# Queries computed for two heads at once, and score maxima on two halves of TensorE's rows

## What is computed

```
xn = layernorm(x)
q = (xn @ Wq + bq)          # 16 heads of 64
k, v = xn @ Wk + bk, xn @ Wv + bv   # one key and value head of 64, shared by all 16
w = softmax(q_h . k / 8)    # 512 x 512 for each of 16 heads and 8 batch entries
x = x + concat(w @ v) @ Wo + bo + mixture_of_experts(xn)   # 8 experts, 2 chosen, 512 wide
```

## Time and profile before

| | |
|---|---|
| median of 3 executions | 1417.2 us (1414.25 to 1417.55) |
| the profiled execution | 1409.84 us, its span 1408.0 us |
| TensorE busy | 1286.0 us, 91% |
| VectorE busy | 1011.7 us, 72% |
| ScalarE busy | 708.6 us, 50% |
| GpSimd busy | 270.9 us, 19% |
| mean granted TensorE clock | 0.962 |

### The profile page before, as it was taken

One profiled execution on the slowest core, in us unless ns is written; L12 is line 12 of the kernel. 1 busy time (PEld: TensorE's weight loads), 2 busy tenths in 40 slices (PEclk: granted clock), 3 DMA queues, 4 the chain that ended last, 5 costly groups with the idle time before them and its releaser, 6 DMA issues.

```text
span 1408.0 us, 22235 instructions
## 1 busy us (share of the span) xinstructions
PE 1286.0 (91%) x7377; PEld 760.0 (54%) x7377; DVE 1011.7 (72%) x2393; ACT 708.6 (50%) x1300; POOL 270.9 (19%) x314
## 2 busy tenths in 40 slices
PE   4569988999989998999899999999999979999997
PEld 2335435554545555555454555555655538686844
DVE  7776866578857875787668766876687747677875
ACT  3126544544464445444554445544545448677741
POOL 3033222200120012001200120012000205454630
PEclk9569998999999999999999999999999989999999
DMA  2051433000210021003000200020000246465451
GB/s 75 0 158 61 151 108 138 29 17 19 84 32 17 18 85 32 18 18 85 31 17 19 85 32 17 18 85 32 18 17 19 62 136 207 155 214 170 144 179 48
DMA packets 69299, 100.25 MB, mean 71 GB/s; under 512 B 29196, under 2 KB 45132, under 8 KB 65220
## 3 DMA queue, kind: packets, MB, share of 16 engines
q1 hardware_dynamic: 54628, 66.23, 15.2%
q0 software_dynamic: 11344, 31.64, 6.9%
q10 hardware_dynamic: 3216, 0.97, 0.3%
HBM read 59.86 MB, written 38.68 MB: 70 GB/s over the span
## 4 chain that ended last, share of the span: by engine, by line
PE 73%; DVE 16%; issue 3%; DMA 2%; ACT 2%; SPq 2%; POOL 1%; DVEq 0%; ACTq 0%; POOLq 0%
PE bank L1420 14%; PE bank L1392 8%; PE bank L1348 7%; PE bank L1431 6%; PE bank L1393 6%; PE bank L1256 5%; PE bank L1258 5%; PE bank L1257 5%; PE bank L1452 4%; DVE mneg L987 3%; PE bank L1272 2%; PE bank L1262 2%; DVE q_lm L981 2%; PE bank L1307 2%; PE bank L1289 1%
## 5 line engine op out<-in xcount | busy, mean ns | idle before, releaser
L815 ACT ACTIVATE wide<-bank 128x512 f32<-128x512 f32 x512 | 301.5, 604 | 493.3 <-PE bank L1393 483.0
L987 DVE TENSOR_REDUCE mneg<-bank 128x1 f32<-128x512 f32 x512 | 347.2, 685 | 182.2 <-PE bank L1348 176.5
L1420 PE MATMUL bank<-wide,v_w 128*32 128x512 f32 x2048 | 249.5, 605 | 0.5 <-issue 0.5
L1348 PE MATMUL bank<-k_hl,q_hh 128*128 128x512 f32 x512 | 208.0, 407 | 34.9 <-DVE mneg L987 21.7
L1392 PE MATMUL bank<-q_hh,k_hl 128*128 128x512 f32 x512 | 234.7, 458 | 1.7 <-ACT wide L815 1.4
L1393 PE MATMUL bank<-q_lm,k_h 65*128 65x512 f32 x512 | 203.6, 398 | 0.0
L1392 PEld LDWEIGHTS bank<-q_hh,k_hl 128*128 128x128 f32 x512 | 97.0, 189 | 131.1 <-issue 89.5
L614 POOL TENSOR_TENSOR rs<-rs,power 128x4 f32<-128x4 f32 x24 | 24.6, 1026 | 626.4 <-DVE rs L889 626.4
L1348 PEld LDWEIGHTS bank<-k_hl,q_hh 128*128 128x128 f32 x512 | 98.1, 192 | 72.6 <-issue 51.7
L1431 PE MATMUL bank<-wide,ones 128*32 128x512 f32 x992 | 129.1, 592 | 0.0
L684 POOL DMA_INDIRECT y_rows<-y_m,to_u x92 | 104.2, 1132 | 127.0 <-DVE y_m L1114 105.1
(11 more groups left out here) (231 smaller groups left out, 1970.4 us busy)
## 6 DMA issues: line engine op xcount, KB each, us to landing
w_t<-w_rows SPq DMA_DIRECT2D x23, 1024.0 KB
x_rows<-part_h POOLq DMA_DIRECT2D x65, 258.0 KB, 6.1
inv<-inverse_scratch SPq DMA_DIRECT2D x124, 128.0 KB, 2.9
w_rows<-w_t SPq DMA_DIRECT2D x8, 1024.0 KB, 4.9
x_m<-x_rows SPq DMA_DIRECT2D x23, 258.0 KB, 3.6
stage<-in_L_ffn_W SPq DMA_DIRECT2D x16, 256.0 KB, 5.2
yab<-y_rows POOLq DMA_DIRECT2D x8, 512.0 KB, 9.4
xin<-in_L_attn_x SPq DMA_DIRECT2D x8, 256.0 KB, 5.9
```

The costliest lines, as they stand in the source:

```text
L815: act.activation(wide[:, st.g % WIDE, :], ps, ACT.Exp, scale=SCALE1).then_inc(wide_full, 1)
L987: dve.tensor_reduce(mneg[:, (gh // 2) % 2, col:col + 1], ps[:], X, ALU.max, negate=True)\
L1348: into(("mx", gh, j), lambda ps: pe.matmul(ps[:], q_hh[:, gh % HEADS, P * j:P * j + P], k_hl[:, n % 2, :], start=True, stop=True))
L1420: pe.matmul(ps_out[0][rows, :], v_w[:, n, c, TILE * d:TILE * d + TILE], weights, start=(c == 0), stop=(c == TT - 1))
```

## The change

- A query product is made for two heads: `wq_h` and `wq_l` hold each head once, and head 2p comes out in partitions 0 to 63, head 2p+1 in 64 to 127. There are 64 query products and not 128. All three matmuls of one come at s2 (`QUERY_AT`), not at s1 and s5.
- ScalarE rounds the two halves separately, each only into its own half of `q_hh`. Four steps later, at s6, it copies each to the other half (`copy_q`), since `first` still needs the query in both. That is 128 new ScalarE instructions of 64 x 512.
- VectorE's `lo_q` handles both heads, at s3, now ahead of that step's pieces of layer 0.
- The maxima are made two tiles at a time, for the two heads of a pair, at the even steps: each is a matmul over 64 rows, one on partitions 0 to 63 (`k_h1`), the other on 64 to 127 (`k_hh`, a new copy of the rounded keys, one more ScalarE instruction for each batch entry). They go to two banks. The rest of the keys is left out of the scores for the maximum.
- The second part of the output projection moves from k = 17 to k = 18 of the next batch entry.

The core of the diff:

```
-    LEAD = 3
+    QUERY_AT = 2
-    WO_AT = [ATT - 10, ATT + 17]
+    WO_AT = [ATT - 10, ATT + 18]
...
+        here, total = gh // 2, H // 2 * NB
+        if s == TT + 1 and 0 <= here + 1 < total:
+            events.append(("mt", here + 1))
+        if s == QUERY_AT and 0 <= here + 2 < total:
+            events.append(("q", here + 2))
+        if s % 2 == 0:
+            pair, j = (here + 1, s // 2 + 2) if s < TT else (here + 2, s // 2 - 2)
+            if 0 <= pair < total:
+                events.append(("mx", pair, j))
...
+            def round_q(pair):
+                ps, _ = filled(act, ("q", pair))
+                for b in range(2):
+                    gh, rows = 2 * pair + b, slice(DK * b, DK * b + DK)
+                    if gh >= HEADS:
+                        act.wait_ge(first_full, last_step(gh - HEADS) + 1)
+                    act.activation(q_hh[rows, gh % HEADS, :], ps[rows, :], ACT.Identity, bias=bq[rows, gh % H:gh % H + 1])\
+                       .then_inc(qh_done, 1)
+
+            def copy_q(pair):
+                for b in range(2):
+                    gh, here = 2 * pair + b, slice(DK * b, DK * b + DK)
+                    act.wait_ge(qh_done, gh + 1)
+                    act.activation(q_hh[DK - DK * b:P - DK * b, gh % HEADS, :], q_hh[here, gh % HEADS, :].bitcast(F32), ACT.Identity)\
+                       .then_inc(q_copied, 1)
...
+            def lo_q(pair):
+                ps, free = full(("q", pair))
+                for b in range(2):
+                    gh, rows = 2 * pair + b, slice(DK * b, DK * b + DK)
+                    h, i = gh % H, gh % HEADS
+                    dve.wait_ge(qh_done, gh + 1)
+                    ins = dve.scalar_tensor_tensor(q_lm[0:DK, i, :], ps[rows, :], bq[rows, h:h + 1],
+                                                   q_hh[rows, i, :].bitcast(F32), ALU.add, ALU.subtract)
+                ins.then_inc(free, 1)
...
+            def scores_for_maximum(pair, j):
+
+                n = 2 * pair // H
+                if 2 * pair % H == 0 and j == 0:
+                    read_out(pe, ("k", n))
+                pe.wait_ge(qh_done, 2 * pair + 2)
+                for b, keys in enumerate((k_h1, k_hh)):
+                    gh, rows = 2 * pair + b, slice(DK * b, DK * b + DK)
+                    into(("mx", gh, j), lambda ps: pe.matmul(ps[:], q_hh[rows, gh % HEADS, P * j:P * j + P],
+                                                             keys[rows, n % 2, :], start=True, stop=True))
```

More of the change, by code:

```diff
@@ L211, in head_events, with split_pair, copy_pair, head_uses @@
         gh, events = H * st.r + 2 * p, []
[L212 to L218, removed]
-        return events
-    def split_head(st):
-        if st.kind not in ("pre", "o") or st.k % TT != 2:
-            return None
-        gh = H * st.r + 2 * (st.k // PAIR) + LEAD + 1 + st.k % PAIR // TT
-        return gh if 0 <= gh < H * NB else None
+        here, total = gh // 2, H // 2 * NB
[7 more added lines that the diff above has]
+                events.append(("mx", pair, j))
+        return events
+    def split_pair(st):
+        if st.kind not in ("pre", "o") or st.k % PAIR != QUERY_AT + 1:
+            return None
+        pair = (H * st.r + 2 * (st.k // PAIR)) // 2 + 2
+        return pair if 0 <= pair < H // 2 * NB else None
+    def copy_pair(st):
+        if st.kind not in ("pre", "o") or st.k % PAIR != QUERY_AT + 4:
+            return None
+        pair = (H * st.r + 2 * (st.k // PAIR)) // 2 + 2
+        return pair if 0 <= pair < H // 2 * NB else None
+    def head_uses(st):
+        return [use for e in head_events(st)
+                for use in ([("mx", 2 * e[1] + b, e[2]) for b in range(2)] if e[0] == "mx" else [e])]
     def wo_at(r, part):
@@ L344, in two_layers @@
         k_hl, k_h1 = sb("k_hl", [P, 2, S], F32R), sb("k_h1", [P, 2, S], F32R)
+        k_hh = sb("k_hh", [P, 2, S], F32R)
         v_w, ones = sb("v_w", [P, 2, TT, DK]), sb("ones", [P, TILE])
@@ L397, in two_layers @@
         m_loaded = [sem(f"m_loaded{i}") for i in range(2)]
+        q_copied = sem("q_copied")
         sums_stored, sums_loaded = [sem(f"sums_stored{i}") for i in range(2)], sem("sums_loaded")
@@ L517, in sums_and_inverses @@
                         load_inverse(pair)
-            where = {}
             def load_tile_weights(t):
@@ L632, in _ @@
                 src = raw[:, n, :].rearrange("p (h d) -> p h d", d=DK)
-                for hi, lo in zip(copies(wq_h[:, 8 * n:8 * n + 8]), copies(wq_l[:, 8 * n:8 * n + 8])):
-                    ins = pool.tensor_tensor(lo, src, hi.bitcast(F32), ALU.subtract)
-                ins.then_inc(split_l, 1)
+                pool.tensor_tensor(wq_l[:, 8 * n:8 * n + 8], src, wq_h[:, 8 * n:8 * n + 8].bitcast(F32), ALU.subtract)\
+                    .then_inc(split_l, 1)
             def zero(n):
@@ L802, in _ @@
                         src = raw[:, n, :].rearrange("p (h d) -> p h d", d=DK)
-                        for hi in copies(wq_h[:, 8 * n:8 * n + 8]):
-                            last = act.activation(hi, src, ACT.Identity)
-                        last.then_inc(split_h, 1)
+                        act.activation(wq_h[:, 8 * n:8 * n + 8], src, ACT.Identity).then_inc(split_h, 1)
             act.wait_ge(split_l, 2)
@@ L829, in _ @@
                         store_m(event[1])
+                if copy_pair(st) is not None:
+                    copy_q(copy_pair(st))
                 for _, n, s in l0_events(st):
@@ L975, in l0, with maximum @@
                 yield from norm(xr[:, :, 0:P], xres[:, n, :, :], lambda ins: ins.then_inc(x1_done, 1), 28)
[L977 to L988, removed]
+            def lo_q(pair):
[7 more added lines that the diff above has]
+                ins.then_inc(free, 1)
+            def maximum(pair, j):
+                for b in range(2):
+                    ps, free = full(("mx", 2 * pair + b, j))
+                    col = TT * b + j
+                    dve.tensor_reduce(mneg[:, pair % 2, col:col + 1], ps[:], X, ALU.max, negate=True).then_inc(free, 1)
             over_e = lambda t: t.unsqueeze(2).to_broadcast([P, TT, E])
@@ L1207, in _ @@
             for st in steps:
+                if split_pair(st) is not None:
+                    lo_q(split_pair(st))
                 if st.kind in ("pre", "o"):
@@ L1211, in _ @@
                             next(cuts[n], None)
-                if split_head(st) is not None:
-                    lo_q(split_head(st))
                 for event in head_events(st):
@@ L1334, in twice, with query @@
                 return w.rearrange("p t d -> p (t d)")
-            def query(gh):
-                n, h = divmod(gh, H)
+            def query(pair):
+                n, h = divmod(2 * pair, H)
                 if h == 0:
                     read_out(pe, ("xt", n))
[L1340 to L1345, removed]
-                    read_out(pe, ("k", n))
-                pe.wait_ge(qh_done, gh + 1)
-                into(("mx", gh, j), lambda ps: pe.matmul(ps[:], q_hh[:, gh % HEADS, P * j:P * j + P], k_hl[:, n % 2, :],
-                                                         start=True, stop=True))
+                into(("q", pair), lambda ps: three(ps[:], twice(wq_h[:, h:h + 2]), twice(wq_l[:, h:h + 2]),
+                                                   x_h[:, n % 2, :], x_l[:, n % 2, :]))
+            def scores_for_maximum(pair, j):
+                n = 2 * pair // H
+                if 2 * pair % H == 0 and j == 0:
+                    read_out(pe, ("k", n))
+                pe.wait_ge(qh_done, 2 * pair + 2)
[3 more added lines that the diff above has]
+                                                             keys[rows, n % 2, :], start=True, stop=True))
             def turn_maxima(pair):
@@ L1388, in first @@
                     if c == 0:
-                        read_out(pe, ("q", gh))
+                        if gh % 2 == 0:
+                            read_out(pe, ("q", gh // 2))
+                            pe.wait_ge(q_copied, gh + 2)
                         pe.wait_ge(m_loaded[(gh // 2) % 2], (gh // 4 + 1) * 16)
```

11 lines of the change are left out of this document (3 added, 8 removed).

## The result

The changed kernel takes 1568.0 us (median of 4, 1565.3 to 1576.8), the kernel before 1415.7 in the same comparison. The ratio is 1.109, 95% interval 1.104 to 1.114: 152 us slower. The forecast was 1454 in a range of 1395 to 1482. The direction was right and the size four times too small.

What follows compares the result with a forecast made beforehand. TensorE was taken to bound the kernel. +24.5 us for entries 0 to 6 and +12.8 for the last gave +37 on 1409.8, so 1447, or 1454 carried to the median; range 1395 to 1482.

Steps and rivals of the forecast that it cites:

- 5.16: Length in us from the start of s2 to s5 in a pair without other work, 2.41 before.
- the 80 us that I gave the maxima's line: TensorE's maxima matmuls waiting for q_lm: about 1.6 us in most pairs, some 80 us in total.
- my 34: 256 couples of maxima on row tiles cost 0.60 us each against 0.47: 34 us more on TensorE.
- -14.6: Steps s1 and s5, which keep only values, get shorter by 1.8 us a pair, eight pairs an entry.
- the sum had 45: On TensorE, 64 pairs lose three query matmuls each, 192 x 0.235 = 45 us saved.
- the sum had 3.5: Growth of each of batch entries 0 to 6: +3.5 us, x 7 = +24.5.
- rival 4: The new waits lower TensorE's granted clock: two drops an entry, +16 us, 1470; chance 0.15 together with another rival.
- I had 12.8: Growth of the last entry, without layer 0 work: seven bare pairs at +1.9 us and one covered at -0.5.
- 14.5: Growth of s2 to s4 in us over the eight pairs of an entry, other work covering parts.
- 4.3: Growth of s6 to s0 in us over the eight pairs of an entry, the last pair 1.2.
- -0.4 (hidden-layer matmuls at k = 59 already wait today): The last pair's s2 to s4 get 0.4 us shorter, as the hidden-layer matmuls there wait already.
- The copies' term of +1.0 in a bare pair: Two copies at s6 delay the exponential of s7 and the next s1: +1.0 us where nothing else fills s0.

Runs made afterwards that it cites:

- e4: The kernel before, with each maximum's matmul over rows 0 to 63 and not 128, still one per step: 1554.5 us, ratio 1.101.
- e6: The changed kernel with the query and the copies at s1 and the maxima over 128 rows, without row tiles: 1354.5 us, ratio 0.960.
- e2: The changed kernel with six spare matmuls before the first tile of s4 in five of eight pairs: 1523.2 us, ratio 1.082.
- e3: The changed kernel with the copies at s5 and not at s6: 1532.2 us, ratio 1.087.
- e1: The changed kernel with the query at s1 and not s2, so lo_q at s2 and the copies at s5: 1386.9 us, ratio 0.983.
- e5: The changed kernel with both lo_q at s2, ahead of the maxima on VectorE, and not at s3: 1548.5 us, ratio 1.097.
- e7: The changed kernel with both lo_q at s2, ahead of the maxima, and the copies at s5: 1547.7 us, ratio 1.097.
- e9: The changed kernel with the six spare matmuls at s4 and the copies at s5 together: 1535.4 us, ratio 1.087.

## Why the prediction was right or wrong

**Right.** TensorE bounds the kernel and the maxima must wait for the query's bank at s4: s2 to s5 in 5.15 us against 5.16, and 5.08 in the first pair of the last entry. The waits are there, if smaller than the 80 us that I gave the maxima's line: 58.0 on it in 43 waits, 83.5 with the other lines. The row tiles cost what the column tiles show: 0.33 us in and 0.43 out, close to the sum, and e4 and e6 confirm the sign and roughly the size (25 us for 256 couples, my 34). The values steps shrank: with the clock restored (e2) s1 and s5 lose 15.3 us an entry beyond the moved projection, against -14.6. The savings of the paired query are real, e6 has them: 57 us, of which the sum had 45; k = 59, where TensorE had waited for the query's bank, gives 9 us over the entries (6.7 to 4.7 in the mean of 1 to 5), most of the rest.

**Right by luck.** The last entry grew by 12.9 us, and I had 12.8. But two of the seven bare pairs counted there make no query at all, since none is left to make (s2 to s4 2.52 and 2.40); the six others lost more than they were given.

**Wrong: the clock.** Each of the entries 1 to 5 grew by 22.1 us (143.2 to 165.4), where the sum had 3.5. The step that failed first is rival 4, "each drop adds about a microsecond: two an entry, +16". I had one drop an entry on record, after 1.4 us of idleness, saw that the new waits were 1.65, and yet put the drops in a rival with two an entry and at nothing in the sum. Measured: eight separate stretches of low clock in entry 3, where the rival had two new ones; 2 x (1 - 0.901) x 1568 = 310 us of low clock against 107 before, 34 us in an entry against 3; and 1.7 us lost for a drop that falls on `values`. e2 gives back 45 us with all waits in place, 57 with the 12 that its fillers cost at k = 52, and still keeps 168 us of low clock. An upper estimate is half of the 203 us that were added, 101.

**Wrong: the cover in pairs with other work.** The sum had +3.5 an entry. With most of the clock drops gone (e2) it is +14.0 (157.3 against 143.2), or 12.4 without the filler's own 1.6. s2 to s4 grew by 20.8 beyond the projection, 19.2 without the filler, where I had 14.5; s6 to s0 by 8.5 where I had 4.3. The worst term is "-0.4 (hidden-layer matmuls at k = 59 already wait today)", measured +2.2: they wait for the query's bank longer than before, when the longest wait there was 1.4.

```profile
759.08 0.48 PE L1423 MATMUL bank<-q_hh,k_hl 128*128 128x512 f32 x1
...
762.64 4.51 PE L1298 MATMUL bank<-x0t,w 128*128 128x512 f32 x6 [2.85 <-DVE q_lm L1006]
```

Their wait is 2.85, and s3 at k = 59 takes 7.4 us; before it took 6.7, and with the query at s1 it takes 4.4. In s6 to s0 three terms were short. At k = 30 to 32 it is 2.6 for 0.45, because a wait of 1.3 us for a maximum's bank that stood at k = 33 now comes at k = 32 (1.4); what it adds here it takes from s1. At k = 46 to 48 it is 1.1 for 0.15. In the last pair I had 1.2: the copies stand ahead of layer 0's L731 there, and with the low clock the changed kernel loses 4.1, 3.3 of them by the copies (e3). The copies' term of +1.0 in a bare pair was too large: nothing at k = 40, where other work at s6 covers them, 0.55 in the last entry.

**The account.** The savings of the pairing (45) and the price of the row tiles (25) are in e1 too, and e1 is 24 us faster than before. So the place of the query costs 181 us, and not only the 152 by which the kernel grew. In entries 1 to 5 the changed kernel takes 165.4 us, e2 157.3 and e1 141.1, a difference of 24.3 from the first to the last. The filler gave back 8.1 of it, 9.7 with its own 1.6: the clock. s3 and s4 are 12.4 longer in e2 than in e1 once that 1.6 is off: the waits for the query's bank. 2.2 are left. Entries 0 to 6 together hold 166 of the 181. The 21 us at k = 62 and 63 that the copies bring lie in both parts. How the parts divide is an estimate and no more, for e5, e7 and e9 show that these costs do not add: removing one moves the clock drops.

## What to carry to other kernels

Put a chain of small dependent steps (round, subtract, free the bank) under the longest stretch of the bounding engine that does not need it; the query at s1 and not at s2, with the copies one step earlier, was worth 181 us. Where a wait can bring the granted clock down, count it twice: the wait itself, and then the matmuls behind it at the low clock. Two row tiles for one change of tiling are dearer than two matmuls over the full array (25 us for 256 couples); whether more of them in a row would pay, no run here shows.

## What had not been expected of the hardware

- 240 useless matmuls, most of them in idle time, made the kernel 45 us faster (1568.0 to 1523.2), through the clock alone: the waits stayed (s4 takes 2.79 us with them and 2.80 without).
- The clock makes local gains non-additive: 45 and 36 us alone, 33 us together (1568.0 to 1535.4).
- A matmul over 64 rows between two over the full array costs 0.28 us more than one over 128 rows, over 512 of them; one over 65 rows costs no more than one over 128.
